# Norms of a two-layer hybrid transformer on one core: eight tile operations become one or two over all tiles

## The reference, cut to what matters

```python
def _layernorm(x, axis=-1, eps=1e-05):
    m = jnp.mean(x, axis=axis, keepdims=True)
    v = jnp.var(x, axis=axis, keepdims=True)
    return (x - m) / jnp.sqrt(v + eps)

x = x + attention_full(_layernorm(x))          # 16 heads, no mask
x = x + ffn(_layernorm(x))
x = x + causal_then_local(_layernorm(x))       # two attentions with rms norms, on h = _layernorm(x)
x = x + ffn(_layernorm(x))
x = x + attention_window32(_layernorm(x))
x = x + experts(_layernorm(x))                 # 2 of 8 experts for each token, rms norm inside
x = x + attention_window128_sinks(_layernorm(x))
x = x + experts(_layernorm(x))
```

## Time and profile before

| | |
|---|---|
| median of 3 runs | 2767.42 us (2761.36 to 2775.89) |
| profiled execution | 2760.11 us |
| its span, first to last instruction | 2758.3 us |
| mean granted TensorE clock | 0.918 |
| PE busy | 2298.4 us, 83% |
| DVE busy | 1628.1 us, 59%, 3443 instructions |
| ACT busy | 1443.7 us, 52% |
| POOL busy | 623.3 us, 23% |

### The profile page before, as it was taken

The page is one execution under the profiler, slowest core; times in us unless marked ns, Lnnn a source line. Parts: engine busy times, 40 slices in busy tenths (PEclk is TensorE's granted clock), DMA queues, the critical chain, the costliest instruction groups (busy, mean ns, idle before and its releaser), DMA issues.

```text
span 2758.3 us, 49767 instructions
## 1 busy us (share of the span) xinstructions
PE 2298.4 (83%) x19922; PEld 1234.8 (45%) x19922; DVE 1628.1 (59%) x3443; ACT 1443.7 (52%) x2121; POOL 623.3 (23%) x533
## 2 busy tenths in 40 slices
PE   5488898898899999998999899868886878948883
PEld 2011231232222335444435575535784756736873
DVE  7988878888885314326615644754473836634442
ACT  1067767767788887764586354322333334413331
POOL 2400000020010203223212412342115241243224
PEclk7599999999999999998999999988987889978996
DMA  4600101011010112012112342143534352514663
GB/s 149 205 14 21 40 14 47 23 45 35 23 48 20 46 35 72 25 44 89 48 54 51 118 142 86 35 130 104 152 114 140 95 172 60 160 47 153 190 185 100
DMA packets 162221, 229.56 MB, mean 83 GB/s; under 512 B 19264, under 2 KB 86336, under 8 KB 161736
## 3 DMA queue, kind: packets, MB, share of 16 engines
q1 hardware_dynamic: 148776, 205.91, 25.3%
q0 software_dynamic: 8192, 16.79, 2.0%
q10 hardware_dynamic: 5024, 3.67, 0.4%
HBM read 151.90 MB, written 74.95 MB: 82 GB/s over the span
## 4 chain that ended last, share of the span: by engine, by line
PE 55%; DVE 21%; issue 6%; ACT 5%; another core or an unknown queue 4%; DMA 4%; POOL 3%; SPq 2%; ACTq 0%; POOLq 0%; DVEq 0%
PE PS L1120 12%; DVE MS L1505 12%; PE PS L1169 8%; PE PS L1103 7%; PE PS L1074 7%; PE PS L1085 5%; PE PS L1186 4%; ACT PT L1276 4%; PE PS L965 2%; PE PS L1004 2%; PE PS L994 2%; PE PS L1130 2%; DVE XN L1372 1%; SPq L1738 1%
## 5 line engine op out<-in xcount | busy, mean ns | idle before, releaser
L1276 ACT ACTIVATE PT<-PS 128x1024 f32<-128x1024 f32 (+5 forms) x1216 | 1028.5, 905 | 535.2 <-PE PS L1103 472.6
L1505 DVE TENSOR_REDUCE MS<-PS 128x2 f32<-128x1024 f32 (+3 forms) x736 | 785.9, 1100 | 336.8 <-PE PS L1085 211.1
L1120 PE MATMUL PS<-PT,VA 128*9 128x512 f32 (+10 forms) x6720 | 570.4, 439 | 17.0 <-issue 9.2
L1103 PE MATMUL PS<-QO,KO 51*128 51x512 bf16 (+13 forms) x3360 | 437.8, 305 | 47.1 <-DVE MS L1505 21.5
L1074 PE MATMUL PS<-c_half 128*128 128x128 bf16 (+4 forms) x1472 | 326.8, 305 | 107.1 <-DVE MS L1505 65.0
L1085 PE MATMUL PS<-KO,QO 48*128 48x512 bf16 (+3 forms) x1984 | 304.6, 332 | 106.5 <-DVE MS L1505 79.6
L1169 PE MATMUL PS<-SG,WB 128*128 128x128 f32 x2208 | 297.5, 288 | 20.8 <-issue 8.7
L1085 PEld LDWEIGHTS PS<-KO,QO 48*128 48x128 bf16 (+1 forms) x1984 | 112.9, 98 | 430.4 <-DVE MS L1505 226.7
L1103 PEld LDWEIGHTS PS<-QO,KO 51*128 51x128 bf16 (+4 forms) x3360 | 150.7, 95 | 317.0 <-issue 121.9
L1169 PEld LDWEIGHTS PS<-SG,WB 128*128 128x128 f32 x2208 | 277.8, 202 | 28.9 <-issue 27.3
L1298 ACT ACTIVATE HM<-PS 128x384 f32<-128x384 f32 x184 | 90.4, 491 | 259.6 <-PE PS L1169 231.1
(11 more groups left out here) (155 smaller groups left out, 2265.7 us busy)
## 6 DMA issues: line engine op xcount, KB each, us to landing
WB<-in_mW SPq DMA_DIRECT2D x184, 384.0 KB
scr_o<-SG SPq DMA_DIRECT2D x40, 256.0 KB
PT<-scr_y SPq DMA_DIRECT2D x16, 512.0 KB, 5.3
KO<-scr_k_full SPq DMA_DIRECT2D x32, 204.0 KB
QO<-scr_q_full SPq DMA_DIRECT2D x32, 192.0 KB
scr_q_causal<-PQ SPq DMA_DIRECT2D x24, 256.0 KB
QO<-scr_q_causal SPq DMA_DIRECT2D x32, 192.0 KB
scr_q_local<-PQ SPq DMA_DIRECT2D x24, 256.0 KB
```

The costliest lines, as they stand in the source:

```text
L1103: p = mm(pb[0:kn, h2, at:at + tn], k[:, k0:k0 + kn], q[:, t0:t0 + tn], start=not masked, stop=True, skip_group_check=masked)
L1120: p = mm(bank[32 * h:32 * h + D + 1, c0:c0 + tn], va[0:kn, :], pt[0:kn, h % 2, at:at + tn], start=s["first"] and j == 0, stop=s["last"] an ...
L1276: e = activation(pt[0:r, :, a:b], ps[0:r, :, a:b], ACT.Exp, scale=s["A"].scale)
L1505: v.tensor_reduce(to, got, AX.X, ALU.max).then_inc(S["top"], 1)
```

## The change

The eight instructions of a norm become two `tensor_tensor` over all eight tiles. The first subtracts the mean, the second multiplies by the root in place; mean and root are views repeated 128 times along the row (a step of zero). Between the two VectorE waits until the first has written (`settled`). The eight instructions of the scaled rows become one `tensor_tensor`.

```diff
                 w.wait_all(s.needs["v"])
                 w.wait_all(s.use["dst"].after)
-                for i in range(NT):
-                    a = v.tensor_scalar(dst[:, i, :], src[:, i, :], MV[b][:, i, 0:1], RS[b][:, s["at"] + i:s["at"] + i + 1], ALU.subtract, ALU.mult)
-                a.then_inc(S["norm"], 1)
+                rows = [128, NT, 128]
+                last(v.tensor_tensor(dst[:, :, :], src[:, :, :], MV[b][:, :, 0:1].broadcast_to(rows), ALU.subtract))
+                settled()
+                v.tensor_tensor(dst[:, :, :], dst[:, :, :], RS[b][:, s["at"]:s["at"] + NT].unsqueeze(2).broadcast_to(rows), ALU.mult).then_inc(S["norm"], 1)
 
             def scaled(s):
...
-                for i in range(NT):
-                    a = v.tensor_scalar(XN[:, i, :], h[:, i, :], RS[b][:, i:i + 1], None, ALU.mult)
-                a.then_inc(S["scaled"], 1)
+                v.tensor_tensor(XN[:, :, :], h[:, :, :], RS[b][:, 0:NT].unsqueeze(2).broadcast_to([128, NT, 128]), ALU.mult).then_inc(S["scaled"], 1)
```

## The result

| | before | after |
|---|---|---|
| median of 19 runs each, us | 2765.40 (2755.55 to 2775.89) | 2777.62 (2769.62 to 2787.14) |
| ratio, 95% interval | | 1.0045 [1.0035, 1.0055], +12.2 us |
| profiled execution, its span, us | 2760.11, 2758.3 | 2781.33, 2779.5 |
| mean granted TensorE clock | 0.918 | 0.917 |
| PE, DVE, ACT, POOL busy, us | 2298.4, 1628.1, 1443.7, 623.3 | 2297.5, 1639.6, 1444.2, 629.1 |

The change makes the kernel slower by 0.45%, three times the forecast of 4 us. The two profiled executions are 21 us apart, and the medians 12. Single runs of one kernel differ by 18 to 20 us, so the medians carry the size, and the traces are read for the places.

A forecast was written before the change was run, and what follows sets the result against it. PE held 55% of the chain, DVE 21%. Norms +4.9, scaled step -0.4, norm at 1246 -2.2, roots +0.9, other norms +1: about +4 us, 2764 by the profiled run, named 2770; range 2755 to 2785.

The forecast's parts named there:

- One norm: Each of 44 norms on DVE: hold from 2.05 to 2.40 us, 0.35 us more; 14 on the chain add 4.9 us.
- A scaled step: Each of four scaled steps on DVE: 1.65 us becomes 1.23, 0.42 less; one on the chain, -0.4 us.
- Meetings with POOL: Six norms stretched beside two-operand POOL instructions: stretching persists; the one at 1246 us falls from 6.76 to about 4.6, -2.2 us.
- The rule that I had weighed: DVE instructions with two SBUF inputs and GpSimd ones reading SBUF contend; the first issued blocks the other for its whole length.
- The roots: POOL's roots at 1478 us, behind the 1.23 us scaled step, begin a good 1 us later; +0.9 us booked.
- The 29 other norms: Norms off the chain add between nothing and 10.2 us; taken as 1 us because other work ended later.
- The path counted at 15 norms: The chain before, followed piece by piece, passes through 15 of the 44 norms, from 14 to 2546 us.
- Everything lands: Rival: all 44 norms push what ends last, about +12.4 us, 2772 us or 2779 by the average; chance 0.12.
- New meetings: Rival: POOL takes its turn in the norm's added wait; seven more meetings, +18 us, 2778 or 2784; chance 0.10.
- Meetings lost: Rival: the shift ends all six norm meetings and shortens stretched casts, about -14 us, 2746 or 2752; chance 0.08.
- a form that does not meet POOL: Rival: the new norm operations never contend with POOL, -9 us, 2751 or 2757 by the average; chance 0.04.
- The half-rate operand: Repeated norm operand read at half rate: 2.3 us per operation, norm 2.1 longer, 32 us on chain; nearly excluded.

The follow-up runs named there:

- e12: Only the four scaled steps as one operation each, norms as before, against the kernel before: 2762.59 us, ratio 1.0012 [1.0000, 1.0025].
- e8: Kernel before with each norm as four operations over two tiles each, values not the reference's: 2574.85 us, ratio 0.9961 against the kernel before, -10.1 us.
- e4_late: The change in the last 24 norms only, scaled steps as before, against the kernel before: 2597.48 us, ratio 1.0049, +12.7 us.
- e3_early: The change in the first 20 norms only, scaled steps as before, against the kernel before: 2588.56 us, ratio 1.0012, +3.1 us.
- e9: The whole changed kernel run again, against the kernel before on the same chip: 2769.64 us, ratio 1.0048, +13.2 us.
- e10: The kernel before, unchanged, submitted as a null against itself: 2757.23 us, ratio 1.0006 [0.9992, 1.0019].

## Why the prediction was right and where it was wrong

The range held by its width, and the ratio is within the half percent that I had given most of the chance, near its edge. But 2777.6 us lies 7.6 above the forecast, the effect is +12.2 us (interval 9.7 to 15.2) where I had +4, and so many runs tell it from no change.

- *One norm.* Right. 2.40 us of hold and an end at 2.49 us were predicted and measured. A repeated column costs nothing: 1225 ns. Instructions 3151 as said; DVE busy +11.5 us (predicted about 12).
- *A scaled step.* Right in duration, 1.23 us. Its 1.7 us are below what `e12` can measure.
- *Meetings with POOL.* They persist, with either engine held by the other: 4.40 us near 1127 (predicted about 4.3), 4.29 near 1248 (predicted 4.6). The rule that I had weighed, in the Trainium skill, page "SBUF — State Buffer", section "Who interferes with whom", the trace confirms: POOL's operation of 0.29 us was held for 1.23. The roots came 0.8 us late (1.63 - 0.81), where I had booked 0.9.
- *"The 29 other norms add between nothing and 10.2 us; I take 1, because something else ended later at each of them."* This is the step that failed. It put 1 us on 10.2 us of added time; the runs show that added time costs about 0.5 us or more per us, wherever it is added, so 5 us or more. The cover is thin at many norms: with 0.35 us 19 and 21 of them are on the chain instead of 15 and 16, with 1.28 us 32. I had read cover from the share of busy time, and a busy PE says nothing of how much later than the norm its work ends. The path counted at 15 norms is closer to what shortening them brings: 15 x 0.76 = 11.4 us, where `e8` gained 10.1.
- *The clock.* No step of mine had it. At one place a pause of PE that grew by 1.25 us was followed by a lower granted clock, and the next norm came 5 us later. The same 5 us stand in every trace in which that norm is longer, by 0.35 or by 1.28. They make most of why the small dose seems to land nearly in full and why `e4_late` costs more than `e3_early`; the gain of the norm near 1248 us, which falls in the early half, widens the gap between the two.
- *The rivals.* "Everything lands" named +12.4 us, and that size came, by a different way, so the match is luck: the first 20 norms cost 3.1 us of their 7.0, and the late part more than its own length. New meetings: one norm, near 1773 us, is newly stretched, by 0.9 us (its first operation took 2.17, in `e9` the same), and not seven. Meetings lost, and a form that does not meet POOL: neither happened.
- *Slips in the working.* The half-rate operand was called 2.1 us longer per norm, but that is against the new form's 2.40 us; against the norm as it was (2.05) it is 2.5, so 37 us over 15 norms and not 32. Nothing in the forecast hung on it.

What can be counted: of the 19 norms on the chain, those near 1248 and 1484 us stand apart, and 17 x 0.35 = 6.0; scaled -0.4; the norm near 1248 -2.5; the roots +0.8; the new stretch near 1773 us +0.9; the place near 1484 us +5.1 (the mean of after and e9, less that of before and e10). Together 9.9 us, against 12.2 and 13.2 measured. The remaining 2.3 to 3.3 us stay open. Over the whole run the mean clock of `e9` is 0.9160 and that of before beside it 0.9179, at the small end of the fall that I had expected (0.002 to 0.004), which is 12 us more at 1.2 GHz (twice the loss of clock, times the run: 465 against 453 us); how much of that makes time and how much goes with waiting that was there anyway, no run here separates.

That the pause lowered the clock is read from the order of events and from the fourteen traces; a run that fills this pause with matmuls was not tried.

## What to carry to other kernels

Fewer instructions are not less time: eight small operations held VectorE 2.05 us and two large ones 2.40, and that has to be read from the trace, for the hold, not from counts or from the mean of a single one. The chain's share tells at most what shortening brings. Lengthening this in-order engine cost 0.5 to 0.8 us per us added, and more where the matrix engine's clock fell; in another kernel a fill of known length ahead of the step measures it in one run. Take such fills away from steps that meet GpSimd, or count what they hide. Look also for the places where the matrix engine already pauses for a microsecond behind that engine: here a little more there came with a lower clock and 5 us.

## What the runs showed of the hardware that was not expected

- The same kernel, unchanged, takes 2585.6 us on the chips of the first two groups and 2758.4 us on that of the third. The first 1480 us are nearly equal (the norm near 1482 us starts at 1479.4 in `e4_late`, which is the kernel before up to there, and at 1482.6 in `e10`); the rest differs. Windows of the rest, columns as above, `e3_early`, which is the kernel before from there on, on a faster chip:

```profile
1480.00:2582.00 1102.00, 974.84 (x9555) 759.18 (x9599) 670.20 (x1858) 449.83 (x857) 404.94 (x371) 0.94 0.46 138
```

  and `e10_before_again` on the slower:

```profile
1480.00:2758.00 1278.00, 1032.60 (x9642) 789.15 (x9642) 668.11 (x1859) 450.52 (x861) 405.95 (x371) 0.88 0.40 119
```

  The same bytes flow at 119 instead of 138 GB/s. What makes the difference was not studied; times from two chips can't be compared for this kernel, only ratios on one.
- Of the eight operations with two numbers per partition each starts 256 ns after the last; over two tiles (`e8`) 323 ns for twice the elements; with one number per partition (the scaled step before) 196 ns. A fill of 320 bfloat16 elements with its wait holds DVE 0.36 us alone, and three of them 1.28.
